# Causal mask of the fourth attention by one-hot rows in the relative scores' product instead of VectorE's minimum, with new ranks for the third chain

## What is computed

```python
x = _layernorm(x + _L3_attn_ref(x, ...))                  # the fourth layer begins
x = _layernorm(x + _L3_xattn_ref(x, ctx_1024, ctx_1024, mask, ...))
x = _layernorm(x + _L3_ffn_ref(x, ...))                   # 8 experts, 2 for each token
```

```python
scores = jnp.einsum('bhqd,bhkd->bhqk', q, k)
rel_idx = pos[None, :] - pos[:, None] + (n - 1)
rel = rel_emb[rel_idx]
scores = scores + jnp.einsum('bhld,lrd->bhlr', q, rel)
causal = pos[None, :] > pos[:, None]
scores = jnp.where(causal[None, None], -jnp.inf, scores)
attn = jax.nn.softmax(scores / np.sqrt(HD).astype(np.float32), axis=-1)
```

## Time and profile before

| | us |
|---|---|
| median of 3 runs | 778.73 |
| lowest and highest | 774.83, 782.65 |
| span of the profiled execution | 780.6 |
| PE, DVE, ACT, POOL busy | 663.0, 549.0, 444.9, 442.9 |

### The profile page before, as it was taken

The page is one execution under the profiler, slowest core; times in us unless marked ns, Lnnn a source line. Parts: engine busy times, 40 slices in busy tenths (PEclk is TensorE's granted clock), DMA queues, the critical chain, the costliest instruction groups (busy, mean ns, idle before and its releaser), DMA issues.

```text
span 780.6 us, 22984 instructions
## 1 busy us (share of the span) xinstructions
PE 663.0 (85%) x8876; PEld 497.6 (64%) x8876; DVE 549.0 (70%) x1471; ACT 444.9 (57%) x1092; POOL 442.9 (57%) x614
## 2 busy tenths in 40 slices
PE   5988896889999996999978989878988889949990
PEld 2665663567777784776456667738955567736990
DVE  4867867976888766787398999543557799952654
ACT  2225644578788763667465767355727667622671
POOL 2258836985777733333155988344666668553550
PEclk8558966999999996899998999688999999957995
DMA  9139000000000000000008600004115481013112
GB/s 298 33 138 229 9 3 0 2 2 2 2 2 3 2 2 1 3 3 3 2 3 139 189 3 4 2 28 99 45 53 180 158 263 43 3 52 91 56 37 88
DMA packets 50793, 44.30 MB, mean 57 GB/s; under 512 B 15904, under 2 KB 41376, under 8 KB 50176
## 3 DMA queue, kind: packets, MB, share of 16 engines
q1 hardware_dynamic: 48448, 38.24, 17.9%
q0 software_dynamic: 2240, 4.60, 1.7%
HBM read 29.95 MB, written 12.88 MB: 55 GB/s over the span
## 4 chain that ended last, share of the span: by engine, by line
PE 55%; DVE 16%; issue 9%; POOL 7%; ACT 6%; DMA 4%; SPq 1%; DVEq 0%; ACTq 0%; POOLq 0%
PE bank L1002 5%; PE bank L981 5%; PE bank L989 4%; PE bank L1070 3%; PE bank L1187 3%; PE bank L1262 3%; PE bank L1269 3%; PE bank L1095 2%; PE bank L1136 2%; DVE sm L1751 2%; PE bank L1120 2%; PE bank L895 2%; DVE X L1687 2%; DVE mx L1753 2%; ACT pT L1357 2%
## 5 line engine op out<-in xcount | busy, mean ns | idle before, releaser
L2173 POOL TENSOR_TENSOR sm<-sm,mx 128x512 f32<-128x512 f32 x80 | 84.5, 1059 | 36.5 <-DVE mx L1753 36.2
L1353 ACT ACTIVATE pr<-sm 128x512 f32<-128x512 f32 x112 | 70.9, 634 | 31.6 <-POOL sm L2173 26.1
L1357 ACT COPY pT<-bank 128x512 f32<-128x512 f32 x112 | 65.5, 585 | 33.7 <-PE bank L989 32.5
L989 PE MATMUL bank<-W,pr 128*128 128x128 f32 x448 | 74.8, 292 | 8.3 <-ACT pT L1357 6.0
L2140 POOL TENSOR_SCALAR veps<-mv 128x1 f32<-128x1 f32 x104 | 23.5, 226 | 90.9 <-DVE mv L1683 90.6
L2168 POOL TENSOR_TENSOR pairs<-KS,quad 128x512 f32<-128x512 f32 x48 | 51.7, 1077 | 35.5 <-ACT KS L1336 35.3
L981 PE MATMUL bank<-pairs,Q 64*64 64x256 f32 x896 | 67.1, 418 | 3.8 <-DVE sm L1745 2.7
L989 PEld LDWEIGHTS bank<-W,pr 128*128 128x128 f32 x448 | 52.5, 147 | 18.4 <-issue 10.5
L2141 POOL TENSOR_TENSOR rstd<-veps,W 128x1 f32<-128x1 f32 x104 | 58.9, 567 | 8.7
L1002 PEld LDWEIGHTS bank<-VX,pT 64*64 64x64 f32 x3072 | 53.4, 142 | 10.2 <-issue 4.5
L1002 PE MATMUL bank<-VX,pT 64*64 64x9 f32 (+1 forms) x3072 | 56.7, 204 | 1.8 <-ACT pT L1357 1.1
(11 more groups left out here) (399 smaller groups left out, 1850.4 us busy)
## 6 DMA issues: line engine op xcount, KB each, us to landing
big<-gup SPq DMA_DIRECT2D x4, 1024.0 KB, 10.1
rel_scratch<-G SPq DMA_DIRECT2D x16, 256.0 KB, 2.6
W<-small SPq DMA_DIRECT2D x1, 3206.5 KB, 12.7
big<-early SPq DMA_DIRECT2D x2, 1557.0 KB, 8.3
slots_x<-zero SPq DMA_DIRECT2D x2, 1472.0 KB, 21.0
big<-down SPq DMA_DIRECT2D x8, 256.0 KB, 8.9
QM<-rel_scratch SPq DMA_DIRECT2D x16, 128.0 KB, 2.7
PM<-rel_scratch SPq DMA_DIRECT2D x16, 128.0 KB, 2.8
```

Of the source, the lines that this page charges most:

```text
L989: last = pe.transpose(tile(ps, p), pr[:, u % 2, 4 * h + p, :, :].rearrange("p b k -> p (b k)"), ident)
L1353: act.activation(pr[:, u % 2, 4 * h:4 * h + 4, :, :].rearrange("p g b k -> p (g b k)"), sm[:, 2 * (u % 2) + h, :], ACT.Exp, scale=a["scale ...
L1357: act.copy(pT[:, u % 2, 4 * h:4 * h + 4, :], bank[BK[f"tu{h}"]][:, :].rearrange("p (h n) -> p h n", h=4)).then_inc(pt_ready, 1)
L2173: tt(v, v, bc(mx[:, slot, :], [P, 8, S], 2), ALU.subtract).then_inc(pcentered, 1)
```

## The change

The product of the relative scores now makes the mask. A query tile of one half of the heads has zeros in the feature rows of the other half. In those rows each query gets a one at its own position (`spot`), and the second operand (`relc`, in place of `relp`) has there -1e30 for those distances of a head that a query at this position never uses, which are the ones that the shifted read brings to the keys behind it. For the last head of a row the numbers behind it must be -1e30 too: the rows in DRAM get a 513th column, stored once (`beyond`), and the shifted reads go by 512 instead of 511 numbers.

So the minimum goes (16 instructions on DVE). New are: on POOL for each tile of a3 an add (`pool.rq`, 128x256) between `act.q` and `pe.rel`; in `rel_rows` ten DVE operations that build the tables; the fill of `beyond` on POOL at the program's start, and its store from SP behind the zero fills. The products, copies, stores and reads keep their number and size; the stored rows start 2,052 bytes apart instead of 2,048. `CHAIN_RANK` has new numbers throughout.

```diff
-              "act.rel": -2.0, "pe.in": -12.0, "act.in": 9.5, "pool.kv": -1.0, "act.q": -8.0, "act.x": -2.0,
+              "act.q": -1.25, "act.x": -23.0, "act.out": -11.75, "pe.dn": -12.5, "dve.scan": 1.75, "pe.q": 0.5,
...
-            rows += [("pe.rel", 0, ["act.q"]), ("act.rel", 0, ["pe.rel"]), ("dma.rel", 0, ["act.rel"])]
+            rows += [("pool.rq", 0, ["act.q"]), ("pe.rel", 0, ["pool.rq"]), ("act.rel", 0, ["pe.rel"]), ("dma.rel", 0, ["act.rel"])]
...
-    scratch = nc.dram_tensor("rel_scratch", (MB, P * 512), F32, kind="Internal")
+    scratch = nc.dram_tensor("rel_scratch", (MB, P * 513), F32, kind="Internal")
...
+            sp.wait_ge(rest_in, 16)
+            sp.dma_start(scratch.ap().rearrange("m (p n) -> p m n", n=513)[:, :, 512:513], beyond[:, :].unsqueeze(2),
+                         allow_slow_non_contiguous=True).then_inc(beyond_in, 16)
...
-                    sp.dma_start(scratch.ap()[b].rearrange("(p n) -> p n", n=512),
+                    sp.dma_start(scratch.ap()[b].rearrange("(p n) -> p n", n=513)[:, 0:512],
                                  G[:, b % 4, :]).then_inc(rel_stored[b % 2], 16)
...
-                        skew = bass.AP(tensor=scratch, offset=b * P * 512 + c * S * 512 + S - 1,
-                                       ap=[[511, S], [1, 512]])
+                        skew = bass.AP(tensor=scratch, offset=b * P * 513 + c * S * 513 + S - 1,
+                                       ap=[[512, S], [1, 512]])
...
-                        pe.wait_ge(q_split, at_["q", t])
+                        pe.wait_ge(rq_ready, 8 + t + 1)
+                        pe.wait_ge(relc_ready, 2)
                         for c in range(2):
-                            mm(fill(6 + c, rel_ready)[:, :], own_q[:, c, :],
-                               relp[:, :, :].rearrange("p h k -> p (h k)"), start=True, stop=True).then_inc(rel_full, 1)
+                            mm(fill(6 + c, rel_ready)[:, :], RQ[:, t % 2, c, :, :].rearrange("p b s -> p (b s)"),
+                               relc[:, c, :, :].rearrange("p h k -> p (h k)"), start=True, stop=True).then_inc(rel_full, 1)
...
-                return last
+                link(last)
+                link(dve.tensor_reduce(eighth[:, 0:8], w("ident").rearrange("p (m i) -> p i m", i=8), AX.X, ALU.add))
+                link(tt(own_row.rearrange("p (j i) -> p j i", i=8), bc(w("pair16"), [P, 8, 8], 2), bc(eighth[:, 0:8], [P, 8, 8], 1),
+                        ALU.mult))
+                link(dve.tensor_tensor_scan(behind, ones[:, 0:S], own_row, 0.0, ALU.mult, ALU.add))
+                link(tt(behind, behind, own_row, ALU.subtract))
+                backwards = bass.AP(tensor=behind.tensor, offset=behind.offset + S - 1, ap=[behind.ap[0], [-1, S]])
+                for c in range(2):
+                    ts(spot[:, c, :], own_row, w("par16", 1 - c, 2 - c), None, ALU.mult)
+                    last = ts(early_keys[:, c, :], backwards, w("par16", 1 - c, 2 - c), -1e30, ALU.mult, ALU.mult)
+                link(last)
+                for c in range(2):
+                    last = stt(relc[:, c, :, :], relp[:, :, :], w("par16", c, c + 1), bc(early_keys[:, c, :], [P, 8, S], 1),
+                               ALU.mult, ALU.add)
+                last.then_inc(relc_ready, 1)
...
-                                link(tt(dst, dst, bc(w("causal"), [P, 8, S], 1), ALU.min))
...
+                    if step == "rq":
+                        if t >= 2:
+                            pool.wait_ge(rel_full, 2 * (t - 1))
+                        pool.wait_ge(q_split, q_count(name, t))
+                        pool.wait_ge(relc_ready, 2)
+                        tt(RQ[:, t % 2, :, :, :], Q[:, q_slot(name, t), :, :].rearrange("p c (b s) -> p c b s", b=2),
+                           bc(spot, [P, 2, 2, S], 2), ALU.add).then_inc(rq_ready, 1)
```

More of the change, by code:

```diff
@@ L181 @@
               5, "up1": 2, "dn": 4, "lg": 0, "rk": 6}
-CHAIN_RANK = {"pe.sc": 2.5, "pe.v": 9.5, "pe.tu": -5.0, "pe.rel": -11.0, "dve.mix": 6.0, "act.ex": 11.5, "pe.va": 3.0,
-              "pe.y": -2.5, "pe.x": -0.5, "dve.re": 5.5, "pool.xb": 19.5, "dve.on": 0.5, "act.k": -9.0, "act.o": -8.0,
-              "dve.v": -10.5, "pe.up": -13.0, "pool.ce": -1.0, "act.pt": -4.0, "pe.fo": -3.5, "act.up": 4.5,
-              "act.rel": -2.0, "pe.in": -12.0, "act.in": 9.5, "pool.kv": -1.0, "act.q": -8.0, "act.x": -2.0,
-              "act.out": -7.5, "pe.dn": -3.0, "dve.scan": -6.5, "pe.q": -1.5, "pe.k": -2.0, "dve.fi": -9.5, "pool.rs":
-              2.0, "dve.sc": -6.5, "pe.lg": -2.5, "dve.e1": 1.5, "pe.rk": 5.0, "dve.e2": 14.0, "dve.sl": 10.5,
-              "act.lg": -7.5}
+CHAIN_RANK = {"pe.sc": 9.25, "pe.v": 11.25, "pe.tu": -14.25, "pe.rel": -12.0, "dve.mix": 1.5, "act.ex": 27.0,
+              "pe.va": -2.0, "pe.y": -11.25, "pe.x": 8.0, "dve.re": 12.75, "pool.xb": 38.5, "dve.on": -3.5,
+              "act.k": -21.0, "act.o": -34.0, "dve.v": -11.0, "pe.up": -0.75, "pool.ce": -38.75, "act.pt": -17.0,
+              "pe.fo": -6.25, "act.up": -5.0, "act.rel": 8.25, "pe.in": 2.25, "act.in": 14.75, "pool.kv": -11.75,
+              "act.q": -1.25, "act.x": -23.0, "act.out": -11.75, "pe.dn": -12.5, "dve.scan": 1.75, "pe.q": 0.5,
+              "pe.k": 1.0, "dve.fi": -7.5, "pool.rs": 28.0, "dve.sc": -7.25, "pe.lg": 7.75, "dve.e1": -8.75,
+              "pe.rk": 10.5, "dve.e2": 10.25, "dve.sl": 34.0, "act.lg": -15.0, "pool.rq": -24.5}
 MIDDLE_RANK = {"pe.sc": 0.0, "pe.v": 2.0, "pe.tu": -3.5, "pe.rel": -11.0, "dve.mix": 10.5, "act.ex": 11.0, "pe.va":
@@ L246 @@
     ("pe.v", "pe.va", 6, 4), ("pe.va", "pe.fo", 4, 2), ("pe.fo", "pe.y", 2, 2), ("dve.re", "dve.fi", 4, 4),
-    ("dve.mix", "dve.scan", 4, 4), ("pe.in", "ema.y", 4, 4), ("act.rel", "dma.rel", 2, 2), ("dma.rel", "a3.sc", 2, 2)]
+    ("dve.mix", "dve.scan", 4, 4), ("pe.in", "ema.y", 4, 4), ("act.rel", "dma.rel", 2, 2), ("dma.rel", "a3.sc", 2, 2), ("pool.rq", "pe.rel", 2, 2)]
 def place(name, t):
@@ L443, in decoder @@
         relp = sb("relp", [P, 8, S])
+        beyond = sb("beyond", [P, MB])
         bqm = sb("bqm", [P, 6, 2])
@@ L550, in decoder @@
         e3_w = room(0, NE3 * WIDE3, "p (e n) -> p e n", e=NE3)
+        relc = room(NE3 * WIDE3, 2 * 512, "p (c h k) -> p c h k", c=2, h=8)
+        RQ = room(NE3 * WIDE3 + 2 * 512, 2 * 256, "p (j c b s) -> p j c b s", j=2, c=2, b=2)
+        early_keys = room(NE3 * WIDE3 + 3 * 512, 2 * S, "p (c k) -> p c k", c=2)
+        spot = room(NE3 * WIDE3 + 3 * 512 + 2 * S, 2 * S, "p (c s) -> p c s", c=2)
+        own_row, behind, eighth = (room(NE3 * WIDE3 + 3 * 512 + (4 + i) * S, S, "p n -> p n") for i in range(3))
         keys3 = cap[:, 0].rearrange("p b k -> p (b k)")
@@ L629, in decoder @@
         acc_ready, row_added = (sem(n) for n in ("acc_ready", "row_added"))
+        beyond_in, relc_ready, rq_ready = rest_in, mixed_ready, vj_ready
         att = {
@@ L691, in decoder, with q_count @@
         planned = [chain_plan(stages)[0] for stages in CHAINS]
+        def q_count(name, t):
+            queries = [(n, i) for part in planned for s, n, _, i, _, _ in part["act"] if s == "q"]
+            return queries.index((name, t)) + 1
         def order_in(engine, step, n):
@@ L775, in _ @@
                              back_y[HALF * hh:HALF * (hh + 1), :].rearrange("(t p) n -> p t n", p=P)).then_inc(gathered, 16)
+            sp.wait_ge(beyond_in, 32)
             for t in range(MT):
@@ L1982, in context3 @@
                 four = lambda v, n: v.rearrange("p (t h d) -> p t h d", t=n, d=8)
-                dve.wait_ge(pool_init, 5)
+                dve.wait_ge(pool_init, 6)
                 dve.wait_ge(v_full, due(v_full))
@@ L2096, in _ @@
             top1_ffn()
-            link(rel_rows())
+            rel_rows()
             mask_x3()
@@ L2116, in _ @@
             n_init = 0
-            for v, number in ((VX[:, :, :, 8:9], 1.0), (VX32[:, :, :, 4:5], 1.0), (HT[:, :, 0:1], 0.0), (zero[:, :], 0.0)):
+            for v, number in ((VX[:, :, :, 8:9], 1.0), (VX32[:, :, :, 4:5], 1.0), (HT[:, :, 0:1], 0.0), (zero[:, :], 0.0), (beyond[:, :], -1e30)):
                 pool.memset(v, number).then_inc(pool_init, 1)
```

4 lines of the change are left out of this document (2 added, 2 removed).

## The result

The changed kernel took 791.42 us in the median of six runs (786.23 to 793.32), the kernel before 784.25 in six. The ratio is 1.0153, with a 95% interval from 1.0118 to 1.0188: about 1.5% slower. 772 us was forecast, 0.8% faster, and a loss of over 1% had a chance of 0.11. The profiled execution took 790.8 us, 10.2 more than before. (All ratios here are formed from undisturbed runs alone and so are not the quotients of the medians beside them (here 1.0091), and the profiles of e1_pitch and e11_nomin are of disturbed runs.)

A forecast was written before the change was run, and what follows sets the result against it. SP's 5.6 us round was taken to pace the fourth attention, held where products wait for VectorE. 780.6 - 6.5 = 774.1 us profiled, median forecast 772.2, said as 772; own range 768 to 777, widened to 764.5 to 780.5.

The forecast's parts named there:

- What bounds the stage: Fourth attention: SP's 5.6 us round of stores, landing and reads paces tiles, except where products wait for VectorE.
- The rest: Side effects outside the main sum: constant column, stores, GpSimd's fill and first chain, each taken as zero.
- the term for the stores: Relative-score stores at 2,052-byte pitch: no change from 2.9 us; 3.5 as bound, 3.6 us lost on six rounds.
- rival C: Shifted rows lengthen each store: gain gone at 1.1 us more, 787 at 2.5 more; chance 0.09.
- The rounds: SP's store-to-store rounds, tile 1 to tile 7: six of 5.6 us, putting tile 7's store at 623.2.
- The head of the chain: Third chain's start: tables delay the copy 2.5 us, second y 2.3 us, first store 1.0 us.
- rival B: TensorE's clock falls in the gap before the filler: filler 3.6 us longer, gain 3.0, 775.7; chance 0.14.
- SP's first round swallows the late start: Between stores 0 and 1: 1.0 us late start absorbed, so tile 1 stores as now, near 589.6.
- The end of the stage: Tile 7's store to its first add 8.0 us, then 5.0 to x3's first score step at 636.2.
- rival D: Minima were not on the path, or a product stands behind something overlooked: gain 0.5, 778; chance 0.09.
- The gain itself: x3's first score step at 636.2 instead of 642.74: gain 6.5 us from the fourth attention's stage.
- What was set to nothing: Constant column, x3 and experts zero; first chain zero, plus or minus 2 us; query adds hidden from tile 2.

The follow-up runs named there:

- e1_pitch: Kernel before with only the scratch layout of the change (rows 2,052 bytes apart, filled cell, reads skewed by 512): ratio to before 1.0053 (0.9991 to 1.0114).
- e11_nomin: Repeat, in five rounds, of the kernel before without VectorE's sixteen minima and nothing in their place (causal mask left out): ratio to before 0.9927 (0.9887 to 0.9968).
- second profile: Profile of the changed kernel measured again, unedited: 789.83 us (before 782.47), ratio to before 1.0100 (1.0044 to 1.0157).
- e8_nomin: Kernel before without VectorE's sixteen minima and nothing in their place (causal mask of the fourth attention left out): ratio to before 0.9981 (0.9937 to 1.0024).
- e12_ranks_before: Kernel before with nothing changed but the ranks of the changed kernel: 784.74 us (before 782.47), ratio 1.0027 (0.9986 to 1.0068).
- e10: Changed kernel again, unedited, rows 2,052 bytes apart: 789.83 us (before 782.47), ratio 1.0100 (1.0044 to 1.0157).
- e3: Changed kernel with the third chain's old ranks (-10 for the new query step), rows 2,052 bytes apart: 791.44 us, ratio to before 1.0105.
- e4: Changed kernel with VectorE's tables built behind the copy that frees bank 2, rows 2,052 bytes apart: 785.12 us, ratio to before 1.0007.
- e2_pad640: Changed kernel with only the scratch rows wider, 2,560 bytes apart (640 elements): 777.97 us (before 782.08), ratio 0.9917 (0.9878 to 0.9955).
- e5: Changed kernel with rows 2,112 bytes apart (528 elements): 778.86 us, ratio to before 0.9950 (0.9902 to 0.9999).
- e9: Changed kernel with rows 2,080 bytes apart (520 elements): 780.24 us, ratio to before 0.9965 (0.9926 to 1.0005).
- e6: Changed kernel with rows 2,560 bytes apart and VectorE's tables behind the copy that frees bank 2: 777.84 us, ratio to before 0.9969.

## Why the prediction was wrong

**What bounds the stage** was read rightly: SP's round of store, landing, reads and next store sets the pace, the break at tile 4 goes, VectorE then waits for reads. That is also why a repeated term weighed so much.

**The step that failed** is in "The rest", the term for the stores: "I take no change from 2.9". An edit that lengthens every round was set to nothing. Over the eight tiles the wait measured 3.72 us (3.75 in the second profile) where it had been 2.66, and the landing 3.9 where it had been 2.6. The reason given was "2 x 1,472 KB in 21.0 us, by which 256 KB take 1.9 us, not above the 2.0". That row is a rate, and it cannot hold this cost: the windows above show the pair's data moved in the same 1.8 us at all three pitches, and the extra time behind that. The row was also divided unevenly, two fills in flight together against one store of a pair (the pair would take 3.65 us by it). That this lies so near 3.72 is luck: moving the pair's data took 1.8 us, and the fills themselves took from 21.0 to 28.2 us in the fourteen profiles (25.8 in that of the changed kernel). And the 1.9 us (1.8 by the row) stood below the 2.66 that SP already waited, so the rate left something out before the change as well. Why a landing comes later at this pitch stays open.

The forecast named 3.5 as the bound of a store, and rival C had the mechanism: "from 1.1 us more per store (4.0 instead of 2.9) the gain is gone". Each pair's wait took 1.1 more than before. By that alone the gain would be gone; the rest of the loss is in the parts below. That C was given only 0.09 rests on the same row. The Trainium skill (DMA: Bandwidth & Descriptors, "How a descriptor splits into AXI transactions") has one transaction more for a descriptor that does not start on 256 bytes, which the prediction weighed as an estimate of 0.36 us a store. The runs do not show that price: rows 2,080 and 2,112 bytes apart mostly do not start on 256 bytes, rows 2,560 apart (ten times 256) all start as the first one does, and all three land in 3.0 us; the 2.6 of the kernel before is no measure of it either, since the same pitch of 2,048 landed in 2.9 in e8_nomin and e11_nomin and in 2.2 in e12_ranks_before. Rows 2,052 apart land in 3.8 to 4.2. So the rule pointed against the edit, but it does not tell a pitch of 2,052 from one of 2,080, and the runs do.

**The rounds.** 5.6 us were forecast; with the rows 2,560 bytes apart they are 5.70. The difference of 1.17 (6.87 - 5.70) six times is 7.0 us, most of the 7.6 us lost between store 1 and store 7. The same means lie between 6.6 and 7.0 in the other kernels with the new product and the narrow pitch (e10, e3, e4), and between 5.7 and 6.2 in those with the wider ones.

**The head of the chain.** Counted from the last copy of the experts' results (567.39 before, 567.07 after), the copy came 2.3 us later (2.5 forecast) and the first y 2.3 (2.5 forecast). The second y, forecast 2.3 us late, came 3.6 late: the filler took 4.98 us instead of 3.60, and the granted clock from 574 to 590 is 0.92 instead of 1.00. That is rival B, in part: of the 3.6 us that a filler wholly at the lower level would have cost, 1.4 came. Store 0 came 19.2 us behind that copy, 2.6 later than before (1.0 forecast); but in e8_nomin, whose code up to there is that of before, it is 19.2 too, so this difference is not clearly the change's. To store 1 it took 5.45 us where 4.6 were forecast: here the forecast that SP's first round swallows the late start failed. Little of this is the pitch's, since it takes 5.27 with the rows 2,560 bytes apart.

**The end of the stage.** From store 7 to the add 8.0 were forecast, 11.5 came. In the kernel before it was 10.1 for tile 7 (626.89 to 636.99), and with nothing but the minima taken out 8.2 (e8_nomin and e11_nomin), so 8.0 was a fair price for that. The new steps and their order bring more: 9.9, 11.8 and 12.1 with the rows 2,560, 2,112 and 2,080 bytes apart, so that no part of the 3.5 can be put down to the pitch. In all seven kernels with the new ranks and the new product the last tile's first add waits for a score product on TensorE (0.20 to 1.05 us), not for its read. That is rival D, for this tile alone. The timelines of e2_pad640 show the place, VectorE's first, then TensorE's:

```profile
617.04 0.69 DVE L1775 TENSOR_TENSOR sm<-bank,QM 128x512 f32<-128x512 f32 x1 [2.33 <-DMA QM<-rel_scratch]
...
618.37 0.34 DVE L1717 TENSOR_SCALAR X<-res,mv,rstd 128x128 f32<-128x128 f32 x1
...
635.31 0.69 DVE L1775 TENSOR_TENSOR sm<-bank,PM 128x512 f32<-128x512 f32 x1 [0.20 <-PE bank L997]
```

```profile
618.76 0.33 PE L910 MATMUL bank<-W,X 128*128 128x128 f32 x1 [1.58 <-DVE X L1717]
...
621.55 3.03 PE L986 MATMUL bank<-big 128*128 128x512 f32 x4
...
625.35 1.12 PE L1018 MATMUL bank<-VX,pT 64*64 64x9 f32 x64 [0.55 <-ACT G L1365]
```

The add at 617.04 waits for its read; behind it on VectorE stand the normalised values (line 1717), for them waits a transpose (line 910), behind that on TensorE stands tile 7's product (line 986), and the value products (line 1018) wait for the copy that empties its bank. From there the profile's chain that ended last runs on over TensorE and copies of ScalarE, and the add at 635.31 waits for a score product in it. SP itself is not held by that product: its store at 625.43 follows the reads of tile 6 (623.02, 2.37 to issue) at once.

**The gain itself.** With the rows 2,560 bytes apart the change is worth 0.8% (0.5 to 1.2%), that is 3.5 to 9.5 us, where 6.5 were forecast; in the stage 4.1 (58.7 to 54.6). The other three kernels with the new ranks and a wider pitch (e5, e9, e6) give 0.3 to 0.5%, only one of them clear of none, and stages of 57.5 to 59.3. So the sum without its failed term had the right sign; that its size was right is not shown.

**What was set to nothing** and stayed so: the constant column (landed 22.7 us after its issue, hundreds of us ahead of its use), the first chain (its last residual starts at 115.9 us, before at 115.6; and e12_ranks_before cannot be told from the kernel before), x3 and the experts (137.7 us against 137.9 in the second profile). POOL's query adds lie beside other work but for one wait of TensorE, 0.57 us ahead of a product at 597.00.

## What to carry to other kernels

A rate read from another transfer prices the moving of the data and nothing behind it; here what the pitch cost lay behind it. So hold such a price against what the kernel's own transfer takes now: 1.9 us for a store whose landing already took 2.6 was a sign that the row left something out. A cost inside a round that paces the stage is paid once per round, so an edit that only shifts addresses there needs as much care as the work removed. And a spare column is cheap if it keeps the rows' starts at multiples of 32 bytes: 520 instead of 513 elements turned 1 to 1.5% slower into no slower, and 640 into 0.8% faster, by its ratio the fastest of these kernels (777.97 us beside 782.08).
